# The deformable-convolution stage of a hybrid block: outer products written to PSUM, hats stored tap by tap, 45 instead of 49 stencil taps with flagged corners, far sums added later

## What is computed

```python
xp = x @ in_w + in_b                                  # what is sampled
x1 = silu(batchnorm(depthwise_conv3x3(x)))            # what steers the sampling
offset = x1 @ off_w + off_b                           # 8 groups x 9 points x (x, y) for every pixel
mask = softmax((x1 @ mask_w + mask_b).reshape(..., 8, 9))
# point (kx, ky) of a group samples xp (16 channels) bilinearly at
#   pixel + (kx - 1, ky - 1) + offset
out = sum over the 9 points of mask * sample
return out @ out_w + out_b
```

## Time and profile before

| what | us |
|---|---|
| median of 3 runs | 738.66 (738.63 to 744.75) |
| the profiled execution | 738.27 |
| its span, first to last instruction | 736.4 |
| DVE busy | 580.2 (79%) |
| PE busy | 586.0 (80%) |
| POOL busy | 330.5 (45%) |
| ACT busy | 226.0 (31%) |

### The profile page before, as it was taken

One profiled execution on the slowest core, in us unless ns is written; L12 is line 12 of the kernel. 1 busy time (PEld: TensorE's weight loads), 2 busy tenths in 40 slices (PEclk: granted clock), 3 DMA queues, 4 the chain that ended last, 5 costly groups with the idle time before them and its releaser, 6 DMA issues.

```text
span 736.4 us, 11104 instructions
## 1 busy us (share of the span) xinstructions
PE 586.0 (80%) x3456; PEld 437.0 (59%) x3456; DVE 580.2 (79%) x1052; ACT 226.0 (31%) x332; POOL 330.5 (45%) x326
## 2 busy tenths in 40 slices
PE   5964878877497878297898779978999999948995
PEld 4533556555365556265666557836777777734674
DVE  4588999999479999479999999755777766653666
ACT  6240404206012414210512400024445444423431
POOL 6524855879204879502884867320222111125111
PEclk8996989989699999598998978989999999987998
DMA  6077303003002006000000000000000000004111
GB/s 179 29 293 241 104 1 101 3 1 102 0 1 100 3 1 251 1 0 1 1 2 0 3 1 0 1 1 1 1 0 1 1 1 1 1 2 110 34 44 43
DMA packets 25594, 30.54 MB, mean 41 GB/s; under 512 B 5188, under 2 KB 17684, under 8 KB 25556
## 3 DMA queue, kind: packets, MB, share of 16 engines
q1 hardware_dynamic: 24654, 29.77, 12.3%
q0 software_dynamic: 896, 0.23, 0.3%
q10 hardware_dynamic: 6, 0.00, 0.0%
HBM read 24.94 MB, written 5.05 MB: 41 GB/s over the span
## 4 chain that ended last, share of the span: by engine, by line
PE 46%; POOL 17%; DVE 13%; issue 9%; POOLq 2%; DVEq 1%; ACT 1%; ACTq 0%
PE banks L768 9%; PE banks L879 8%; PE pair L859 8%; DVE prod L1345 5%; POOL got L1080 5%; PE pair L924 4%; PE pair L721 4%; PE banks L869 4%; PE banks L958 3%; DVE stencil L1321 3%; POOL far_list_i L1115 2%; DVE outer L1315 2%; POOL cell_now L1077 1%; POOL pos L1072 1%; PE banks L786 1%
## 5 line engine op out<-in xcount | busy, mean ns | idle before, releaser
L768 PE MATMUL banks<-ident,prod 128*128 128x128 f32 x1568 | 228.9, 298 | 78.0 <-DVE prod L1345 76.7
L768 PEld LDWEIGHTS banks<-ident,prod 128*128 128x128 f32 x1568 | 194.4, 154 | 133.0 <-DVE prod L1345 110.1
L1345 DVE TENSOR_TENSOR prod<-shifted,stencil 128x1024 f32 (+1 forms) x224 | 238.3, 1084 | 36.6 <-PE banks L768 36.6
L1115 POOL CAST far_list_i<-far_list 1x8 int32<-1x8 f32 x8 | 52.2, 6527 | 125.3 <-DVE far_list L1331 113.1
L721 PE MATMUL pair<-xg,dw_diag 128*128 128x512 f32 x144 | 73.2, 610 | 1.2 <-ACT dw_diag L508 1.2
L1143 POOL TENSOR_TENSOR rstd_now<-mv_now,neg_half 128x2 f32<-128x2 f32 x32 | 22.9, 717 | 109.5 <-DVE mv_now L1398 109.5
L879 PE MATMUL banks<-shifted 128*128 128x128 f32 x512 | 63.3, 277 | 2.6 <-ACT shifted L630 1.4
L879 PEld LDWEIGHTS banks<-shifted 128*128 128x128 f32 x512 | 60.2, 192 | 8.4 <-issue 6.5
L1315 DVE TENSOR_TENSOR outer<-hats 128x800 f32<-128x800 f32 x64 | 63.6, 993 | 0.8
L1321 DVE TENSOR_TENSOR stencil<-stencil,outer 128x800 f32 (+1 forms) x64 | 63.3, 990 | 0.3
L859 PE MATMUL pair<-shifted 128*128 128x512 f32 x128 | 60.4, 596 | 0.6 <-ACT shifted L613 0.6
(11 more groups left out here) (229 smaller groups left out, 829.0 us busy)
## 6 DMA issues: line engine op xcount, KB each, us to landing
shifted<-padded SPq DMA_DIRECT2D x42, 256.0 KB, 4.1
shifted<-padded SPq DMA_DIRECT2D x14, 640.0 KB, 8.0
res<-in_x_dram SPq DMA_DIRECT2D x4, 512.0 KB, 5.9
padded<-stage SPq DMA_DIRECT2D x4, 512.0 KB, 2.6
stage<-in_L_ffn_W_dram SPq DMA_DIRECT2D x16, 128.0 KB, 2.1
out_dram<-res SPq DMA_DIRECT2D x8, 256.0 KB, 2.3
padded<-stencil SPq DMA_DIRECT2D x2, 228.0 KB, 2.6
got<-padded,cell_now POOLq DMA_INDIRECT x28, 3.0
```

The costliest lines, as they stand in the source:

```text
L768: mm = pe.matmul(acc_of(c, r), prod[:, d % PROD, r * G:(r + 1) * G, :].rearrange("p g c -> p (g c)"), ident[:, :], is_transpose=True, star ...
L1115: gp.tensor_copy(far_list_i[:, :], far_list[:, :]).then_inc(point, 1)
L1345: ins = ve.tensor_tensor(prod[:, dx:dx + n, :, :], shifted[:, dx:dx + n, bass.ds(((c % HALF) * ROWS + dy) * G, ROWS * G), :], stencil_of[: ...
```

## The change

- **Outer products in PSUM.** `outer` is no longer an SBUF tile but 800 words of PSUM banks 2 and 3. The sums of the taps move to banks 0 and 1 (`acc_of`), and `project` writes into the bank that its chunk has freed.
- **Hats tap by tap.** `hats` is [partition, axis, tap, row x group x point]: each Abs writes 288 neighbouring elements per axis, and the outer product reads the taps of a point at a distance of 288 elements.
- **45 near taps.** The four corners of the 7 x 7 window are left out of `TAP_AT`. The rows of the window come in the order 1, 0, 2, 3, 6, 4, 5. A chunk has 26 units, 19 of two taps and 7 of one.
- **Corner flags.** The four corner points of the 3 x 3 kernel are built first (`POINT_ORDER`). After them DVE sets `at_corner` where a stencil corner is above zero (`flag_corners`); such a column is now a far column too, and `add_point` gathers its corner sample. It has 27 small instructions instead of 22.
- **Far flags by Sign.** ACT's Square and DVE's maximum and comparison go. ACT writes Sign(offset - 2) and Sign(-offset - 2) as bf16 (two instructions of 576 elements), and `count_far` adds these and the corner flags with six matmuls of one output row.
- **Later.** `add_fix` stands ahead of tap 33 of 45, `count_far` at 36, `project` at 40. ACT's `silu` of a chunk runs one turn earlier, behind `prepare`.
- Some tiles move: `samp_t` into `xg`, `bias_parts` into `signs`.

```diff
+ROW_ORDER = (1, 0, 2, 3, 6, 4, 5)
+TAP_AT = [(dy, dx) for dy in ROW_ORDER for dx in range(WIN) if not (dy in (0, WIN - 1) and dx in (0, WIN - 1))]
+NEAR = len(TAP_AT)
+UNIT_AT = [(t, 2 if t + 1 < NEAR and TAP_AT[t + 1] == (dy, dx + 1) else 1)
+           for t, (dy, dx) in enumerate(TAP_AT) if (dx - (dy in (0, WIN - 1))) % 2 == 0]
+UNITS = len(UNIT_AT)
...
-AT_SAMPLES, AT_CONV, AT_FAR, AT_PROJECT = 18, 22, 25, 25
-
-
-STENCIL_FILL = (0, 1, 1, 0, 1, 1, 0, 1, 1)
+AT_CONV, AT_SAMPLES, AT_FAR, AT_PROJECT = 22, 33, 36, 40
+STENCIL_FILL = (0, 1, 1, 1, 1, 1, 0, 0, 0)
+POINT_ORDER = (0, 2, 6, 8, 1, 3, 4, 5, 7)
+CORNERS = 4
...
+def freed_by(tap):
+    dx = TAP_AT[tap][1]
+    before = [t for t in range(tap - NEAR, tap) if TAP_AT[t % NEAR][1] == dx]
+    return before[-1] + 1
...
-        hats = sb("hats", [P, 2, ROWS * GP, TAPS])
-        outer = sb("outer", [P, ROWS * G, TAPS, TAPS])
-        far_xy = outer[:, :, :, :].rearrange("p g a b -> p (g a b)")[:, 0:ROWS * 2 * GP] \
-            .rearrange("p (r o) -> p r o", r=ROWS)
+        hats = sb("hats", [P, 2, TAPS, ROWS * GP])
+        outer = banks[:, 2 * 512:2 * 512 + ROWS * G * TAPS * TAPS].rearrange("p (g a b) -> p g a b", a=TAPS, b=TAPS)
...
                     own(sc.activation(
-                        hats[:, :, :, t].rearrange("p a (r g) -> p a r g", r=ROWS),
+                        hats[:, :, t, :].rearrange("p a (r g) -> p a r g", r=ROWS),
                         off[:, bass.ds(k % OFFS, 1), :, 0:2 * GP].rearrange("p s r (a g) -> p a (s r) g", a=2),
                         ACT.Abs, bias=tap_bias[:, t:t + 1]))
                 own.wait()
-                hf = hats[:, :, :, :].rearrange("p a g t -> p (a g t)")
+                hf = hats[:, :, :, :].rearrange("p a t g -> p (a t g)")
                 sc.activation(hf, hf, ACT.Relu, bias=tap_bias[:, TAPS:TAPS + 1], scale=-1.0).then_inc(hats_done, 1)
+                if not isinstance(k, int) or k > 0:
+                    sc.wait_ge(far_mm, k)
+                    sc.sem_inc(act_waited, 1)
+                for i, sign in enumerate((1.0, -1.0)):
+                    last = sc.activation(signs[:, i, :, :], raw[:, :, 0:2 * GP], ACT.Sign,
...
-                count = pair[1][:, 0:FAR_COLS]
-                pe.matmul(count, ones16[:, :], far[:, :], start=True, stop=False)
-                pe.matmul(count, ones[0:1, :], far_codes[:, :], start=False, stop=True).then_inc(far_mm, 1)
+                count = pair[1][0:1, 0:FAR_COLS]
+                by_corner = count.rearrange("p (g a b) -> p g a b", a=3, b=3)[:, :, 0:3:2, 0:3:2]
+                pe.matmul(count, ones[0:1, 0:1], far_codes[:, :], start=True, stop=False)
+                pe.matmul(by_corner, far_unit[:, :], at_corner[:, :, :, :], start=False, stop=False)
+                for i in range(4):
+                    mm = pe.matmul(count, far_unit[:, :], signs[:, i // 2, :, (i % 2) * GP:(i % 2 + 1) * GP],
+                                   start=False, stop=(i == 3))
+                mm.then_inc(far_mm, 1)
...
             def acc_of(c, r):
-                return bank[1 + 2 * (c % 2)][:, r * P:(r + 1) * P]
+                return bank[c % 2][:, r * P:(r + 1) * P]
...
+                    c, t = k + i // NEAR, i % NEAR
+                    slot = TAP_AT[t][1]
+                    if t == 0 and c >= 2:
+                        pe.wait_ge(res1_done, c)
+                    pe.wait_ge(prod_done, c * NEAR + t + 1)
...
-                add_up(k, AT_SAMPLES, AT_CONV)
-                for i in range(AT_CONV, STENCIL):
-                    if i == AT_PROJECT and not first:
-                        project(k - 1)
+                add_up(k, first_of(BEGIN), AT_CONV)
+                for i in range(AT_CONV, NEAR):
                     if conv_ahead and i == AT_CONV:
                         pe.wait_ge(gate_done, k + 2)
                     if conv_ahead and i < AT_CONV + 9:
                         convolve(k + 2, i - AT_CONV)
                     if i == AT_FAR:
                         count_far(k + 1)
+                    if i == AT_SAMPLES and not first:
+                        add_fix(k - 1)
...
+                step(gp.tensor_tensor(tap_d[:, 1, :], low[:, :], place_mid, ALU.subtract), 8, False)
...
+                step(gp.tensor_tensor(outmost[:, :, :], tap_c[:, 1, :, 0:1].to_broadcast([P, 2, 2]),
+                                      tap_c[:, 1, :, 1].unsqueeze(1).to_broadcast([P, 2, 2]), ALU.mult), 18, False)
+                step(gp.tensor_tensor(within[:, :, :], tap_c[:, 0, :, 0:1].to_broadcast([P, 2, 2]),
+                                      tap_c[:, 0, :, 1].unsqueeze(1).to_broadcast([P, 2, 2]), ALU.mult), 19, True)
+                step(gp.tensor_tensor(outmost[:, :, :], outmost[:, :, :], within[:, :, :], ALU.mult), 20, True)
+                step(gp.tensor_tensor(within[:, :, :], within[:, :, :], outmost[:, :, :], ALU.subtract), 21, True)
+                step(gp.tensor_tensor(within[:, :, :], within[:, :, :], w_now[:, :, :], ALU.mult), 22, True)
+                step(gp.tensor_tensor(w_now[:, :, :], w_now[:, :, :], within[:, :, :], ALU.subtract), 23, True)
...
-                ve.wait_ge(square_done, k + 1)
-                own(ve.tensor_tensor(off_most[:, :].rearrange("p (r g) -> p r g", r=ROWS), far_xy[:, :, 0:GP],
-                                     far_xy[:, :, GP:], ALU.max))
-                fill(1)
-                own.wait()
-                own(ve.tensor_scalar(far_flags, off_most[:, :], float(REACH) ** 2, FAR_UNIT, ALU.is_gt, ALU.mult))
...
+            def flag_corners(k):
+                if not isinstance(k, int) or k > 0:
+                    ve.wait_ge(far_mm, k)
+                    ve.sem_inc(dve_waited, 1)
+                now = stencil_of[:, bass.ds(k % 2, 1), :, :, :].rearrange("p s g a b -> p (s g) a b")
+                ve.tensor_scalar(at_corner[:, :, :, :], now[:, :, 0:WIN:WIN - 1, 0:WIN:WIN - 1].rearrange("p g y x -> p g x y"), 0.0, None, ALU.is_gt
+                                 ).then_inc(corners_done, 1)
             def stencils(k, fill):
                 ve.wait_ge(stencil_clear, k + 1)
-                hx = hats[:, 0, :, :].rearrange("p (g q) t -> p g q t", q=PTS)
-                hy = hats[:, 1, :, :].rearrange("p (g q) t -> p g q t", q=PTS)
+                hx = hats[:, 0, :, :].rearrange("p t (g q) -> p g q t", q=PTS)
+                hy = hats[:, 1, :, :].rearrange("p t (g q) -> p g q t", q=PTS)
                 now = stencil_of[:, bass.ds(k % 2, 1), :, :, :].rearrange("p s g a b -> p (s g) a b")
                 full = [P, ROWS * G, TAPS, TAPS]
-                for q in range(PTS):
+                for i, q in enumerate(POINT_ORDER):
                     kx, ky = q // 3, q % 3
                     to = now[:, :, ky:ky + TAPS, kx:kx + TAPS]
                     own.wait()
-                    own(ve.tensor_tensor(to if q == 0 else outer[:, :, :, :],
+                    if i == CORNERS:
+                        flag_corners(k)
+                    own(ve.tensor_tensor(to if i == 0 else outer[:, :, :, :],
                                          hy[:, :, q, :].unsqueeze(3).to_broadcast(full),
                                          hx[:, :, q, :].unsqueeze(2).to_broadcast(full), ALU.mult))
                     fill(1)
-                    if q > 0:
+                    if i > 0:
                         own.wait()
                         own(ve.tensor_tensor(to, to, outer[:, :, :, :], ALU.add))
-                        fill(STENCIL_FILL[q])
+                        fill(STENCIL_FILL[i])
                 own.wait()
                 ve.sem_inc(hats_used, 1)
...
+                    t, n = UNIT_AT[u]
+                    dy, dx = TAP_AT[t]
...
-                    ve.wait_ge(prod_free, c * STENCIL + d + n)
+                    ve.wait_ge(prod_free, c * NEAR + max(freed_by(t), freed_by(t + n - 1)) + PROD)
```

182 lines of the change are left out of this document (90 added, 92 removed).

## The result

The changed kernel took 769.07 us (median of 4 runs, 766.85 to 778.89) against 741.7 for the kernel before on the same chip (738.63 to 744.92): a ratio of 1.036, 95% interval 1.028 to 1.044. One execution of the four, 778.89, fell into a slower state and is not in the ratio. The direction and the range held; the size did not. The profiled execution took 768.89 us; its span is 767.1 and was 736.4, 30.7 more.

The account below looks back on a forecast made before the run. The prediction took DVE to bound a plain turn and POOL's far sums to add 28 us of waits. DVE's own time +36, waits 28 replaced by 34, last turn +16: +59, giving 797 us, range 745 to 825.

Parts of the forecast that it names:

- chunk 0's stencil: Building chunk 0's stencil with nothing beside it: dearer outer products and corner flags, less earlier ACT hats, +5.6 us.
- DVE's own work in seven turns: DVE's instructions per turn: fewer tap units and flag steps, but nine outer products +6.4 us; a turn 50.6 to 54.9.
- heads of the turns: Where DVE waits for PE at a turn's start: it waits one unit longer less one tap, +0.6 us a turn.
- waits for the far sums: DVE stopped because POOL's sums are late: 28 us before, replaced by 34 (7.8, 13.3 and 13.3).
- last turn: Chunk 6's second point held by DVE's pure product stream, so the last far sums come late: +16 us.
- The hop: Outer product reading the x hat at 1,152-byte steps: 1.90 ns per element, 1.70 us instead of 0.99, +6.4 a turn.
- rival 2: The hop costs its upper bound, 2.10 us per outer product: 29 us more, 826 us; chance 0.12.
- POOL's pace: POOL's time per far point with `outer` in PSUM: 29.5 us, bounds 24 and 36, for 11 points instead of 7.
- Free when reading: Rival 1: a hop is free when reading, a turn is 48.5 us, POOL's waits stay: 750 us; chance 0.13.
- Dearer: Rival 2 by its claim: the outer product's hop costs its upper bound, 2.10 us, 826 us; chance 0.12.
- POOL in time: Rival 4: the hop is paid but POOL's far sums are never late, +5 us, 744 us; chance 0.05.
- the 692 of that rival: Rival 3: hops free and POOL's sums never waited for, a point under 24 us, -46 us; chance 0.06.

Follow-up runs that it names:

- e1: The changed kernel with the hats stored as before, five taps of a point side by side: 730.41 us, 0.985 of the kernel before.
- e4: The kernel before with only the hats stored tap by tap: 778.35 us, 1.049.
- e2: The changed kernel with the outer product written to an SBUF tile again: 802.07 us, 1.087 of the kernel before.
- h1: g2 without the matmul that adds the corner flags to the far counts, leaving out four corner-only points: 714.58 us, 0.964.
- f7: e1 with all 49 taps in natural row order, no corner flags and no corner part of `add_point`: 731.27 us, 0.986.
- h4: h1 with useless matmuls to keep PE busy, 5 behind the 43rd tap and 9 behind the 44th: 709.94 us, 0.955.
- g2: e1 with the window's rows in the order 1, 2, 0, 3, 6, 4, 5: 731.22 us, 0.985.
- g3: e1 with three units begun ahead of a turn instead of two: 733.31 us, 0.989.
- e3: The changed kernel without the matmul adding corner flags to the far counts, so 7 far points instead of 11: 753.89 us, 1.020 of the kernel before.
- f8: e1 with `add_fix` ahead of tap 18 again instead of 33: 752.0 us, 1.011.
- h2: f7 with DVE waiting, behind the last turn's two begun units, until POOL has taken the last list: 723.33 us, 0.976.
- g4: e1 with both edits of g2 and g3, the row order and three units begun: 745.07 us, 1.005.

## Why the forecast was wrong in size

The forecast's chain was list, POOL, far sums, DVE's slots. Its terms against what the traces show, for the 28.4 us at the stage's end:

| term | forecast | measured |
|---|---|---|
| chunk 0's stencil | +5.6 | +6.2 (lists at 63.6 and 69.8) |
| DVE's own work in seven turns, heads and waits apart | 7 x 3.7 = +26 | 7 x 2.9 = +20 |
| heads of the turns | 7 x 0.6 = +4 | 20.2 - 5.6 = +14.7 |
| waits for the far sums | 34 - 28 = +6 | 16.1 - 28.4 = -12.3 |
| last turn | +16 | -0.3 |
| sum | +58 (by the chain 59) | +28 |

- **The hop: right, a little too dear.** The step "1.90 ns per element and stream" came from rows that write, too. Read alone, the hop costs (1552 - 180) / 800 = 1.72 ns: an outer product of 1.55 us, not 1.70. e1 and e4 show both ways round that this is the change's largest cost: 5.1% by e1 (1.036 to 0.985), 4.9% by e4. The Trainium skill's figure for one source hopping 4 KiB (Vector Engine (DVE) Microarchitecture Reference, measured stream behaviour), 1.73 ns, agrees with this trace at a hop of 1,152 bytes. Its 2.50 ns, which the prediction put beside rival 2, the page gives for both sources, or the destination alone, stepping 24 words; here only the x hat hops at every element.
- **POOL's pace: the step that failed.** I took 29.5 us a point between bounds of 24 and 36, counting five more steps against the relief. Measured are 25.4. The relief itself was right (four steps inside an addition, e2 takes it away), but I let only three pass, and charged the five added steps too much: in the point shown two of them took 0.20 us and three were held (1.17, 1.38 and 1.25), and in the next one all five took 0.19 to 0.23. Four us less a point are 12 us less in a chunk of three. With the longer heads, which give POOL time as well, the waits of 7.8, 13.3 and 13.3 became 0, 5.8 and 10.3, and the last turn's 16 went: chunk 6's second point was done at 474.5, as the last turn began, so that no point was left under the pure stream of products. How much of the miss this one term makes is an estimate: the prediction's own chain with 25.4 in place of 29.5, and nothing else changed, has waits of 0, 8.5 and 9.2 us and a last turn of +11, and ends at +38 instead of +59. That is 21 of the 31 us by which the forecast was too high.
- **The Trainium skill's rule on contention** (SBUF — State Buffer, who interferes with whom) says both that DVE with two SBUF inputs contends with GpSimd's reads and that with at most one it does not. I had a row for the first half only and hedged the second with 29.5. The traces agree with both in the building of the stencil: steps of 0.20 us inside the addition, 0.8 us and more in e2. The rule does not say why a cast passes beside a stream of products in one kernel (h1) and not in another (f7).
- **The heads: named, and sized at a quarter.** I counted the missing unit (+0.6) and took PE's own time as unchanged. It isn't: PE stands idle at a turn's end, the granted clock falls (0.50 and 0.56 in the two windows above), and the four taps and the offsets behind it take longer. h4 against h1 shows the part of the clock, g2 against e1 that of the slots.
- **What the forecast didn't see** is that heads and far sums are one account. POOL works on through its seven points of chunks 1 to 3 while DVE waits, wherever it waits; a longer head means a shorter wait behind tap 33. That is why g2 and g3 moved nothing, and h1 did.
- **The rivals.** "Free when reading" (750) fell with e4. "Dearer" (826) fell with the 1.55 us. POOL in time (744) was half right: it was in time in chunks 4 to 6, not in 2 and 3. For the changed kernel to be faster the hop had to be free: e1 (0.985) shows that taking the hop away is enough for that, though not for the 692 of that rival: it stands 24.1 us at the heads and 13.3 us for ACT's hats.

In parts, by single undoings: the hop costs 5% (e1), the corner points 1.6% (e3), and PSUM gives 5% (e2; 3.7% by its lower two executions) in a kernel with eleven points and long outer products; the later place gives 2.6% (f8 against e1); 45 taps with their points give nothing over 49 (f7 against e1), and less than nothing once the last cast of f7 is freed (h2: 0.976).

## What to carry to other kernels

A layout that suits the engine that writes once can cost the engine that reads nine times: price a two-input instruction by how each of its inputs lies in memory, before counting elements. When two waits are served by the same slow helper engine, shortening one lengthens the other; take work off the helper (h1) or give it one gap in a stream that holds it (h2, 26 us of a cast for 1.6 us of waiting). And a pause of TensorE can cost more than its length: behind pauses of 1.1 to 2.6 us at the heads, and of 5.7 us in f7, part of the work here was done at a granted clock of 0.50.

## What the runs showed of the hardware that I had not expected

- A cast of 8 elements on POOL can be held for as long as DVE's products follow each other: the last one took 18.2 us before, 16.8 in e4, 27.9 in f7 and 19.4 in g4, and each time it ended within 0.05 us of DVE's next stop; one stop of 1.6 us made it 2.1 in h2. But in the changed kernel (0.2 us), e1 (0.6), e3, h1 and h4 (1.0 each) it passed amid such a stream without a stop. What decides this stays open.
- DVE's destination in PSUM costs nothing that shows: 999 ns in e1 and 993 before for the same outer product, and 975 against 984 (e2) for the addition that reads it.
- ACT pays for hops when it writes: 1,336 ns by points (e1) and 763 by taps for the same 576 elements.
- Holding grows with the length of the instruction that holds: a point is 30.3 us before and 36.7 in e4, 22.9 in e1 and 25.4 in the changed kernel, where in each pair the outer product is what became longer on DVE.
